# Second attention of a transformer block: where the softmax sums of each head are formed

## The chip, the cores and the metric

The kernel runs on one core of a Trainium2 chip. The metric is the device time of one execution in microseconds (us). The engines of the core work side by side, each through its own instructions in order, and wait for one another on semaphores: TensorE (PE in the profile, with its weight loads as PEld), VectorE (DVE), ScalarE (ACT), GpSimd (POOL) and SyncE (SP), which issues most of the transfers.

## The reference

`x` is 16 batches of 128 tokens of 128 numbers, with a context of 128 tokens of 96 numbers for each batch. Four stages follow one another, each on the layer norm of `x` (the last on `x` itself) and each added to `x`: an attention of 16 heads of 8, a mixture of 8 experts, a second attention of 16 heads of 64, and a mixture of 16 experts. The change is in the second attention:

```python
q_in = x @ Wq + _lora(x, q_down, q_up, q_alpha)
org_ctx = context[:, :end, :]            # 124 tokens
ipa_ctx = context[:, end:, :]            # 4 tokens
k_in = org_ctx @ Wk + _lora(org_ctx, k_down, k_up, k_alpha)
v_in = org_ctx @ Wv + _lora(org_ctx, v_down, v_up, v_alpha)
out = _attention(q_in, k_in, v_in)       # softmax over the 124 keys of each head
out_ipa = _attention(q_in, ipa_k, ipa_v) # softmax over the 4 keys of each head
out = out + IPA_SCALE * out_ipa
return out @ Wo + bo + _lora(out, o_down, o_up, o_alpha)
```

So for each batch, each of 128 queries has 16 rows of 124 powers, each divided by its own sum.

## The kernel before

The program is written engine by engine, with the order of each engine's instructions written out by hand. Every product is in fp32. The second attention runs in rounds, `round1(b)` for b from -1 to 16 (and from -4 on GpSimd, which has less to do in the early ones). A round does several batches at different stages at once: the scores and powers of batch b, the turning, the outputs and the projection of batch t = b - 1, the queries, keys and values of batch f = b + 1, and half of the first mixture's expert products of batch g = b + 4 in each of two places, while there is such a batch (up to b = 11). The rounds from 12 on carry pieces of the second mixture's routing instead: its hidden layer, its top 32 of 128 taken eight at a time (`eight`), and the gathering of rows by one-hot products (`tell`, `onehot`, `gather`, `gathered`).

The 16 heads of a batch are four groups n of CH = 4 heads. Scores of group n lie in PSUM bank n, 4 x 128 columns, of which 124 of each head are the original context and 4 the others. For each group:

- VectorE's `shifted(b, n)` (L755, L756, L758) takes the negated maximum of each head's 124 scores into `negmax1`, and shifts the 4 others into `ipa_s`.
- ScalarE's `powers(b, n)` (L1128) reads the bank and writes `p1`, one activation a head, since each head has its own shift as bias. The last of the four counts up `Z.exp`.
- VectorE's `summed(b, n)` waits for `Z.exp`, reduces the four heads' 496 powers to four sums (L772), waits for that, and takes their reciprocals (L774), which counts up `Z.rsum`.
- GpSimd's `norm(b, n)` (L496) waits for `Z.rsum` and multiplies the four heads' powers by them in place. In the next round TensorE's `turn` (L1491) transposes them, VectorE's `turned` (L766) copies them to `p1T`, and `outputs` (L1521) multiplies them with the values.

In VectorE's round `summed(b, 0)` stands after the second turned group, the other three stand together behind `weighted` (L728), and `ipa_norm` (L779, L781, L783) follows them. `powers` 0 and 1 of a round stand on ScalarE ahead of the copies of the queries (L1135, each after its group) and of `weighted` (L1090, four activations, half of a mixture product); `powers` 2 and 3 stand behind it, then the shifted ones' power (L1218), the outputs' copies (L1141), the keys' copy (L1235), the turned input (L1156) and the values' copies (L1146).

At the end of a round TensorE's projection (L1690) is taken by VectorE's residual (L304), and TensorE's first product of queries (L1500) in the next round, as bank 7 is used again, waits for that by `Z.x_new`. In the rounds b = -1, 3 and 7 (`head_of`) VectorE also does `head_weights` (L709 to L721) ahead of the residual: the choice of two experts for four batches. In the same rounds ScalarE's `head_turned` (L1077) stands behind `powers(b, 0)`, and TensorE's `head_logits` (L1428) waits for it. Rounds b = 2, 6, 10, 11 end with four normalizations in a row (L694, L619).

Of the kernel before, what the change touches and what calls it, by code (L numbers as in the profile page):

```python
# [8 lines left out]
ALU = mybir.AluOpType  # L9
ACT = mybir.ActivationFunctionType  # L10
X = mybir.AxisListType.X
# [9 lines left out]
ORG = S - IPA  # L21
# [6 lines left out]
CH = 4  # L28
# [4 lines left out]
def named(make, prefix, names):  # L33

    return type(prefix, (), {name: make(f"{prefix}_{name}") for name in names.split()})
# [16 lines left out]
def build_program(nc, T, out):  # L52

    with ExitStack() as ctx:
        def sb(name, shape, dt=F32):
            return ctx.enter_context(nc.sbuf_tensor(name, shape, dt))
# [13 lines left out]
        def blocks(b_, rows=128):  # L70
            return b_[0:rows, :].rearrange("p (g n) -> p g n", g=CH)
# [7 lines left out]
        stats = sb("stats", [128, B, 6])  # L79
# [4 lines left out]
        class Arena:  # L84
# [9 lines left out]
            def take(self, shape, dt=F32):  # L94
# [8 lines left out]
                if dt != F32:  # L103
# [71 lines left out]
        p1 = work.take([128, 2, CH, CH, S])  # L175
# [9 lines left out]
        negmax1 = sb("negmax1", [128, 2, H])  # L185
        sums1 = sb("sums1", [128, 2, H])
# [66 lines left out]

        W = named(sem, "w", "turned downT alpha ctx made taken added")
        Z = named(sem, "z", "xn xb tr xT q q_sb k0 k1 k0_sb k1_sb ki v v_sb vi0 vi1 score ipa_max maxed ipa_exp ipa_step ipa_p "
                            "exp sum rsum norm turned p_sb p_odd o o_sb proj x_new stats")

        R = named(sem, "r", "wide count tok picks xn tr xT hid th h logit max ex step topx top turned slot")
        G = named(sem, "g", "told oh got xg")
# [302 lines left out]
        def _(dve):  # L562
# [205 lines left out]
            def summed(b, n):  # L768

                dve.wait_ge(Z.exp, CH * b + n + 1)  # L770
                part = slice(CH * n, CH * n + CH)
                dve.tensor_reduce(sums1[:, b % 2, part], p1[:, b % 2, n, :, 0:ORG], X, ALU.add).then_inc(Z.sum, 1)  # L772
                dve.wait_ge(Z.sum, CH * b + n + 1)
                dve.reciprocal(rsum1[:, b % 2, part], sums1[:, b % 2, part]).then_inc(Z.rsum, 1)  # L774

            def ipa_norm(b):
# [83 lines left out]
            def round1(b):  # L860
# [13 lines left out]
                if there(b):  # L874
                    summed(b, 0)
# [36 lines left out]
                if there(b):  # L912
                    summed(b, 1)
                if b == 15:
                    onehot(3)
                if there(b):
                    summed(b, 2)
                    summed(b, 3)
                    ipa_norm(b)
# [114 lines left out]
        def _(act):  # L1034
# [89 lines left out]
            def powers(b, n):  # L1124

                act.wait_ge(Z.maxed, CH * b + n + 1)
                for c in range(CH):
                    ins = act.activation(p1[:, b % 2, n, c, 0:ORG], blocks(bank[n])[:, c, 0:ORG], ACT.Exp,  # L1128
                                         bias=negmax1[:, b % 2, CH * n + c:CH * n + c + 1])
                ins.then_inc(Z.exp, 1)  # L1130

            def queries(f, n):
# [48 lines left out]
            def round1(b):  # L1181
                f, t, g = b + 1, b - 1, b + 4
                if there(b):
                    powers(b, 0)
# [8 lines left out]
                if there(b):  # L1193
                    powers(b, 1)
# [8 lines left out]
                if there(b):  # L1203
                    powers(b, 2)
# [640 lines left out]
```

## Time and profile before

| | us |
|---|---|
| three runs | 531.68, 531.92, 533.07 |
| median | 531.92 |
| the profiled execution | 532.59 |
| its span in the trace | 530.90 |
| TensorE busy | 495.0 (93%) |
| VectorE busy | 397.5 (75%) |
| ScalarE busy | 272.2 (51%) |
| GpSimd busy | 235.7 (44%) |
| the second attention, rounds 0 to 15 | 141 to 402 on the span |

The profiled execution took 532.59 us; its trace spans 530.90 us of that, so 1.69 us lie around the span. Busy time is the sum of an engine's instructions where they do not overlap. Two instructions that follow one another on ScalarE or VectorE overlap a little, so the start of one to the start of the next (its pitch) is shorter than the duration. The granted clock of TensorE was full (1.00) in the whole second attention.

### The profile page before, as it was taken

Reading aid. Unit: us, or ns where it says so; the run is one execution under the profiler, and the core shown is the slowest. Engines: PE = TensorE matmul, PEld = TensorE weight load, DVE = VectorE, ACT = ScalarE, POOL = GpSimd, SP = SyncE. Lnnn points to the kernel's source line nnn. Section 1 sums busy time; section 2 is a strip of 40 time slices with the busy share of each in tenths; the row PEclk is TensorE's granted clock in tenths of the full one; section 3 lists DMA queues with packets and bytes.
Section 4 is the critical chain, followed back from the end, with each engine's and each line's share of the span. In section 5 each row is a group of like instructions: output and inputs, shape, how many; then the busy total and the mean of one; then the engine's idle time right before and its main releaser. Section 6 shows DMA issues by size and latency. Waiting matters only on the chain.

```text
span 530.9 us, 13371 instructions
## 1 busy us (share of the span) xinstructions
PE 495.0 (93%) x5113; PEld 380.4 (72%) x5113; DVE 397.5 (75%) x1064; ACT 272.2 (51%) x728; POOL 235.7 (44%) x331
## 2 busy tenths in 40 slices
PE   5799998889999998999989999999999999999996
PEld 4467665546567776777768777778857897789895
DVE  6788998556687789777897897777986678536553
ACT  3366564445475564657545665555663544514332
POOL 5844553025365525556255454633312890081440
PEclk9699999899999999999999999999999999999999
DMA  8900000000001101111000000021110400001001
GB/s 227 220 4 4 2 2 2 2 1 7 4 0 32 32 2 33 32 32 32 2 2 1 3 1 3 3 62 45 39 41 1 120 1 2 0 4 41 2 2 41
DMA packets 21871, 14.47 MB, mean 27 GB/s; under 512 B 5928, under 2 KB 21136, under 8 KB 21808
## 3 DMA queue, kind: packets, MB, share of 16 engines
q1 hardware_dynamic: 20704, 13.31, 9.1%
q8 instruction: 42, 0.69, 0.6%
q10 hardware_dynamic: 1104, 0.30, 0.3%
q14 instruction: 21, 0.17, 0.1%
HBM read 12.30 MB, written 1.05 MB: 25 GB/s over the span
## 4 chain that ended last, share of the span: by engine, by line
PE 73%; DVE 20%; issue 3%; ACT 2%; DMA 1%; POOL 0%; SPq 0%; DVEq 0%
PE bank L1758 9%; PE bank L1767 5%; PE bank L1352 5%; PE bank L1521 5%; PE bank L1433 4%; PE bank L1528 4%; PE bank L1508 4%; PE bank L1690 4%; PE bank L1480 4%; PE bank L1500 4%; PE bank L1491 3%; PE bank L1774 3%; PE bank L1337 3%; PE bank L1579 3%; DVE negmax L756 2%
## 5 line engine op out<-in xcount | busy, mean ns | idle before, releaser
L496 POOL TENSOR_TENSOR work<-work,rsum 128x496 f32<-128x496 f32 x64 | 64.2, 1015 | 131.6 <-DVE rsum L774 131.6
L1128 ACT ACTIVATE work<-bank,negmax 128x124 f32<-128x124 f32 x256 | 72.7, 378 | 77.6 <-DVE ipa_s L758 77.6
L531 POOL TENSOR_SCALAR work<-work,slot 128x128 f32<-128x128 f32 x64 | 49.8, 804 | 48.1 <-DVE slot L849 29.3
L1758 PE MATMUL bank<-work 128*128 128x256 f32 x224 | 53.4, 381 | 0.0
L993 DVE SCALAR_TENSOR_TENSOR work<-work,bank 128x256 f32<-128x256 f32 x64 | 26.9, 420 | 32.9 <-ACT work L1280 32.7
L479 POOL TENSOR_TENSOR work<-work 128x512 f32<-128x512 f32 (+2 forms) x48 | 40.3, 839 | 14.1 <-DVE work L728 11.6
L1280 ACT ACTIVATE work<-bank 128x256 f32<-128x256 f32 x64 | 24.6, 384 | 40.5 <-PE bank L1758 29.0
L1758 PEld LDWEIGHTS bank<-work 128*128 128x128 f32 x224 | 40.3, 190 | 4.7 <-DVE work L996 0.2
L430 POOL TENSOR_TENSOR rstd<-veps,minus_half 128x1 f32<-128x1 f32 (+3 forms) x28 | 21.1, 754 | 49.3 <-DVE veps L573 49.2
L756 DVE TENSOR_REDUCE negmax<-bank 128x4 f32<-128x496 f32 x64 | 42.3, 662 | 0.0
L627 DVE TENSOR_REDUCE negmax<-bank 128x8 bf16<-128x1024 f32 x32 | 39.1, 1221 | 4.3 <-PE bank L1322 3.6
L772 DVE TENSOR_REDUCE sums<-work 128x4 f32<-128x496 f32 x64 | 41.4, 647 | 0.5 <-ACT work L1128 0.5
L766 DVE COPY work<-bank 128x512 f32<-128x512 f32 x60 | 40.7, 678 | 0.8 <-PE bank L1491 0.8
L1500 PE MATMUL bank<-xT,work 128*128 128x128 f32 x256 | 34.6, 279 | 7.1 <-DVE x_all L304 4.1
L1480 PEld LDWEIGHTS bank<-work 64*128 64x128 f32 x512 | 31.1, 187 | 13.9 <-issue 8.9
L1491 PE MATMUL bank<-ident,work 128*128 128x128 f32 x256 | 40.1, 279 | 0.3 <-DVE work L783 0.3
L1069 ACT ACTIVATE work<-bank 128x1024 f32<-128x1024 f32 x32 | 31.0, 1022 | 13.8 <-PE bank L1337 13.8
L1480 PE MATMUL bank<-work 64*128 64x128 f32 x512 | 37.2, 285 | 1.0 <-issue 1.0
L1500 PEld LDWEIGHTS bank<-xT,work 128*128 128x128 f32 x256 | 31.1, 192 | 9.4 <-issue 4.7
L1521 PEld LDWEIGHTS bank<-work 128*64 128x64 f32 x512 | 27.4, 136 | 13.2 <-issue 10.4
L1690 PEld LDWEIGHTS bank<-work 128*128 128x128 f32 x256 | 31.0, 191 | 7.4 <-issue 5.1
L1521 PE MATMUL bank<-work 128*64 128x128 f32 x512 | 35.0, 279 | 0.6 <-DVE work L766 0.6
(197 smaller groups left out, 1086.3 us busy)
## 6 DMA issues: line engine op xcount, KB each, us to landing
work<-in_L_ffn_w_dram SPq DMA_DIRECT2D x42, 128.0 KB, 2.3
x_all<-in_x_dram SPq DMA_DIRECT2D x4, 256.0 KB, 5.5
out_dram<-x_all SPq DMA_DIRECT2D x4, 256.0 KB, 2.5
ctx_all<-in_ctx_dram SPq DMA_DIRECT2D x4, 192.0 KB, 5.7
ctx_all<-in_L_ffn_w_dram SPq DMA_DIRECT2D x6, 128.0 KB, 2.2
work<-in_L_xattn_Wq_dram SPq DMA_DIRECT2D x1, 512.0 KB, 6.4
work<-in_L_xattn_Wo_dram SPq DMA_DIRECT2D x1, 512.0 KB, 8.5
work<-in_L_ffn_We_dram SPq DMA_DIRECT2D x1, 512.0 KB, 6.0
```

The lines of the kernel that those rows point to most:

```text
L496: pool.tensor_tensor(part, part, rsum1[:, b % 2, CH * n:CH * n + CH].unsqueeze(2).broadcast_to((128, CH, ORG)), ALU.mult).then_inc(Z.norm, 1)
L531: ins = pool.tensor_scalar(ohw_of(e)[:, k, :], count[:, :], slot[:, h, 0, k, e % E1:e % E1 + 1], slot[:, h, 1, k, e % E1:e % E1 + 1], ALU. ...
L756: dve.tensor_reduce(negmax1[:, b % 2, part], got_s[:, :, 0:ORG], X, ALU.max, negate=True)
L766: dve.tensor_copy(p1T[:, CH * n:CH * n + CH, :], blocks(bank[(4, 6, 5, 4)[n]])).then_inc(Z.p_sb, 1)
L772: dve.tensor_reduce(sums1[:, b % 2, part], p1[:, b % 2, n, :, 0:ORG], X, ALU.add).then_inc(Z.sum, 1)
L1128: ins = act.activation(p1[:, b % 2, n, c, 0:ORG], blocks(bank[n])[:, c, 0:ORG], ACT.Exp, bias=negmax1[:, b % 2, CH * n + c:CH * n + c + 1])
L1480: mm = pe.matmul(blocks(bank[2 * half + odd])[:, c, :], q1T[rows, b % 2, CH * half + c, :], k1T[rows, b % 2, CH * half + c, :], start=True ...
L1491: mm = pe.transpose(blocks(bank[(4, 6, 5, 4)[n]])[:, c, :], p1[:, t % 2, n, c, :], ident[:, :])
L1500: mm = pe.matmul(blocks(bank[5 - n])[:, c, :], wq1[:, part], xT[:, f % 2, :], start=True, stop=True)
L1521: mm = pe.matmul(blocks(bank[5 - n])[D1 * odd:D1 * odd + D1, c, :], v1[:, t % 2, D1 * h:D1 * h + D1], p1T[:, CH * (2 * n + odd) + c, :], s ...
L1690: mm = pe.matmul(bank[7][:, 0:D], o1T[:, c, :], wo1[:, c, :], start=(c == 0), stop=(c == 7))
L1758: mm = pe.matmul(halves(bank[4 + c])[:, n, :], up_weights(e, n, c), xgT[e // E1][:, :, e % E1, :], start=True, stop=True)
```

## The change

Each power's activation gets a second output: `accum_out`, the sum of what it writes along the row, which goes to its head's place in `sums1`. VectorE's reduction of the four heads' powers goes, with the wait for it; the reciprocal of the four sums stays, behind the same wait for `Z.exp`. The semaphore `Z.sum` is dropped. Lines above the edit keep their numbers; L774 becomes L772, and L1128 becomes L1127.

```diff
@@ -769,8 +769,6 @@
                 dve.wait_ge(Z.exp, CH * b + n + 1)
                 part = slice(CH * n, CH * n + CH)
-                dve.tensor_reduce(sums1[:, b % 2, part], p1[:, b % 2, n, :, 0:ORG], X, ALU.add).then_inc(Z.sum, 1)
-                dve.wait_ge(Z.sum, CH * b + n + 1)
                 dve.reciprocal(rsum1[:, b % 2, part], sums1[:, b % 2, part]).then_inc(Z.rsum, 1)
@@ -1125,8 +1123,9 @@
                 act.wait_ge(Z.maxed, CH * b + n + 1)
                 for c in range(CH):
+                    h = CH * n + c
                     ins = act.activation(p1[:, b % 2, n, c, 0:ORG], blocks(bank[n])[:, c, 0:ORG], ACT.Exp,
-                                         bias=negmax1[:, b % 2, CH * n + c:CH * n + c + 1])
+                                         bias=negmax1[:, b % 2, h:h + 1], accum_out=sums1[:, b % 2, h:h + 1])
                 ins.then_inc(Z.exp, 1)
```

VectorE before, from the half mixture product of round 3 to the first step of `head_weights`:

```order
L728 TENSOR_TENSOR work<-bank,work 128x512 [waits f_x_new,f_yb]
L772 TENSOR_REDUCE sums<-work 128x4 [waits z_exp]
L774 RECIPROCAL rsum<-sums 128x4 [waits z_sum]
...
L779 TENSOR_REDUCE ipa_sum<-ipa_s 128x16 [waits z_ipa_exp]
L781 RECIPROCAL ipa_sum<-ipa_sum 128x16 [waits z_ipa_step]
L783 TENSOR_TENSOR work<-ipa_s,ipa_sum 128x16x4 [waits z_ipa_step]
L709 TENSOR_TENSOR work<-work 128x256
```

VectorE in the changed kernel, the same place:

```order
L728 TENSOR_TENSOR work<-bank,work 128x512 [waits f_x_new,f_yb]
L772 RECIPROCAL rsum<-sums 128x4 [waits z_exp] x3
L777 TENSOR_REDUCE ipa_sum<-ipa_s 128x16 [waits z_ipa_exp]
L779 RECIPROCAL ipa_sum<-ipa_sum 128x16 [waits z_ipa_step]
L781 TENSOR_TENSOR work<-ipa_s,ipa_sum 128x16x4 [waits z_ipa_step]
L709 TENSOR_TENSOR work<-work 128x256
```

The three pairs of reduction and reciprocal (two of them behind the dots) have become three reciprocals in a row; nothing else changed places.

ScalarE before, from the first powers of round 1 to the shifted ones' power:

```order
L1128 ACTIVATE work<-bank,negmax 128x124 x4
L1135 ACTIVATE work<-bank 128x512
...
L1090 ACTIVATE work<-bank,work 128x128 x4
L1128 ACTIVATE work<-bank,negmax 128x124 x8
L1218 ACTIVATE ipa_s<-ipa_s 128x64
```

ScalarE in the changed kernel, the same place:

```order
L1127 ACTIVATE work,sums<-bank,negmax 128x124 x4
L1134 ACTIVATE work<-bank 128x512
...
L1088 ACTIVATE work<-bank,work 128x128 x4
L1127 ACTIVATE work,sums<-bank,negmax 128x124 x8
L1217 ACTIVATE ipa_s<-ipa_s 128x64
```

The order and the number of the rows on ScalarE are those of before; the powers have a second output, `sums`.

## Rows read from the trace of the kernel before

**Rows 1.** The page: busy time, share of the span and instructions of each engine.

```profile
PE 495.0 (93%) x5113; PEld 380.4 (72%) x5113; DVE 397.5 (75%) x1064; ACT 272.2 (51%) x728; POOL 235.7 (44%) x331
```

**Rows 2.** Waits of TensorE, 141 to 402 us: total us, times, longest.

```profile
PE bank L1500 <- DVE x_all L304: 4.1, 2, 2.0
PE bank L1500 <- DVE work L766: 3.0, 6, 1.0
PE bank L1428 <- ACT work L1077: 1.5, 2, 0.7
PE bank L1579 <- DVE work L857: 1.3, 2, 0.9
...
PE bank L1491 <- DVE work L783: 0.3, 1, 0.3
```

**Rows 3.** The page's costliest groups: busy us, mean ns of one, idle before.

```profile
L1128 ACT ACTIVATE work<-bank,negmax 128x124 f32<-128x124 f32 x256 | 72.7, 378 | 77.6 <-DVE ipa_s L758 77.6
L772 DVE TENSOR_REDUCE sums<-work 128x4 f32<-128x496 f32 x64 | 41.4, 647 | 0.5 <-ACT work L1128 0.5
```

**Rows 4.** Timeline, VectorE and TensorE, end of round 3: start us, us, instruction.

```profile
196.83 0.66 DVE L772 TENSOR_REDUCE sums<-work 128x4 f32<-128x496 f32 x1
197.52 0.18 DVE L774 RECIPROCAL rsum<-sums 128x4 f32<-128x4 f32 x1
197.61 0.64 DVE L772 TENSOR_REDUCE sums<-work 128x4 f32<-128x496 f32 x1
...
199.15 0.19 DVE L779 TENSOR_REDUCE ipa_sum<-ipa_s 128x16 f32<-128x64 f32 x1
...
206.37 1.16 PE L1500 MATMUL bank<-xT,work 128*128 128x128 f32 x8 [2.05 <-DVE x_all L304]
```

**Rows 5.** Timeline, ScalarE, last powers of round 3; then groups by shape.

```profile
195.16 1.13 ACT L1128 ACTIVATE work<-bank,negmax 128x124 f32<-128x124 f32 x4 [0.21 <-DVE ipa_s L758]
196.17 0.27 ACT L1218 ACTIVATE ipa_s<-ipa_s 128x64 f32<-128x64 f32 x1
196.31 0.24 ACT L1082 ACTIVATE work<-work 128x32 f32<-128x32 f32 x1
...
L1096 ACT ACTIVATE alpha<-alpha 128x4 f32<-128x4 f32 x1 | 0.2, 207 | 0.0
```

**Rows 6.** Timeline, TensorE and ScalarE, round 9, which stands for nine plain ones.

```profile
291.51 1.13 ACT L1128 ACTIVATE work<-bank,negmax 128x124 f32<-128x124 f32 x4 [3.15 <-DVE ipa_s L758]
...
294.45 1.22 ACT L1090 ACTIVATE work<-bank,work 128x128 f32<-128x128 f32 x4
...
297.12 1.02 PE L1433 MATMUL bank<-work 128*128 128x512 f32 x2
...
299.21 0.60 ACT L1141 ACTIVATE work<-bank 128x512 f32<-128x512 f32 x1 [0.33 <-PE bank L1521]
...
301.21 1.12 PE L1528 MATMUL bank<-work,cT_all 96*124 96x512 f32 x2
```

**Rows 7.** Timeline, TensorE, ScalarE, VectorE, round 0.

```profile
146.57 1.21 ACT L1090 ACTIVATE work<-bank,work 128x128 f32<-128x128 f32 x4
...
147.84 1.12 PE L1433 MATMUL bank<-work 128*128 128x512 f32 x2
...
155.61 1.13 PE L1500 MATMUL bank<-xT,work 128*128 128x128 f32 x8 [0.36 <-DVE work L766]
```

**Rows 8.** Timeline, rounds 12, 14 and 15.

```profile
342.24 0.61 ACT L1162 ACTIVATE work<-bank 128x512 f32<-128x512 f32 x1
342.91 1.12 PE L1546 MATMUL bank<-work 128*128 128x512 f32 x2
...
378.50 1.09 PE L1521 MATMUL bank<-work 128*64 128x128 f32 x16 [0.35 <-DVE work L766]
...
395.03 0.62 ACT L1178 ACTIVATE work<-bank 128x512 f32<-128x512 f32 x1
...
396.08 0.38 PE L1571 MATMUL bank<-work,b_pick 128*128 128x512 bf16 x1
```

More of the change, by code:

```diff
@@ L255, in build_program @@
         Z = named(sem, "z", "xn xb tr xT q q_sb k0 k1 k0_sb k1_sb ki v v_sb vi0 vi1 score ipa_max maxed ipa_exp ipa_step ipa_p "
-                            "exp sum rsum norm turned p_sb p_odd o o_sb proj x_new stats")
+                            "exp rsum norm turned p_sb p_odd o o_sb proj x_new stats")
         R = named(sem, "r", "wide count tok picks xn tr xT hid th h logit max ex step topx top turned slot")
```

## The prediction

> **What bounds the kernel now.** The busy shares come first: TensorE is busy 93% of the span, VectorE 75%, ScalarE 51% [rows 1]. A change that moves work from VectorE to ScalarE can thus gain at most TensorE's waits for VectorE, and loses where ScalarE becomes the one waited for. The waits of TensorE in the second attention [rows 2] show what there is. The two largest, 2.05 us each, are L1500 behind VectorE's residual, in the rounds that follow 3 and 7, where VectorE comes late out of its long end of round [rows 4]. Six of 3.0 us in all are for the turned powers' copy L766. These follow the chain projection, residual, norm, maxima, copy, which starts with TensorE's own projection, so an earlier VectorE does not help them, except where VectorE was late for the residual. Two of 0.74 us are L1428 behind ScalarE's L1077, which stands right behind a group of powers: they can only grow. Two of 1.3 us together, in round 15, are gathers behind one-hot rows of VectorE, with sums among its work.
>
> **What goes.** 64 reductions of 647 ns, 41.4 us of VectorE [rows 3]. Most of it lies beside a busy TensorE: in a plain round VectorE waits for the projection at the round's end anyway. It is on the path where VectorE is late:
> - Rounds 3 and 7. From the first of the three late reductions at 196.83 to L779 at 199.15 are 2.32 us [rows 4]. Three reciprocals stay. The row after one starts 0.09 us behind it, and its whole duration is 0.18; I take 3 x 0.18 = 0.54, as each waits on a semaphore. So 1.78 us go, less than the 2.05 that TensorE waits. Behind the residual the L766 wait stays.
> - Round 14: L1521's wait of 0.35 us [rows 8] goes, since the reduction ahead of it in VectorE's queue takes more.
> - Round 15: of the gathers' 1.3 us [rows 2], one reduction, 1.78 / 3 = 0.59 us.
> - Round 0: its waits, 0.28 for L783 [rows 2] and 0.36 for L766 [rows 7], go, 0.64 us.
>
> Sum: 2 x 1.78 + 0.35 + 0.59 + 0.64 = 5.1 us, if the sums cost ScalarE nothing.
>
> **What is added: e, the price of one sum.** No row of before shows an accumulator output. The changed order has the same number of ScalarE's rows, each power with a second output, which would allow e = 0; that the engine needs a step of its own to write 128 single numbers out is as possible. The nearest rows are ScalarE's smallest activations [rows 5]. L1218 (64 elements) starts at 196.17, the next at 196.31: a pitch of 0.14 us, of which the elements are 0.04 to 0.07, as one of 64 takes 0.27 and one of 32 takes 0.24. So about **0.09 us** is what a step with hardly any elements adds in a queue, and that I take. The upper bound: it takes all of L1096's 207 ns and overlaps with nothing, which also loses the 0.12 us by which a power's 378 ns exceeds its pitch of 0.25 (four take 1.01 us from 195.16 to 196.17): e = 0.33. A gain below nothing is excluded, since the powers' own work stays. Per group of four, d = 4e: forecast 0.36, ends 0 and 1.3 us.
>
> The Trainium skill, in "VectorE: DVE Perf Modes", section "Two Vector instructions with no wait between them", says that a VectorE instruction which also writes out its accumulator is two instructions, the second a read of the accumulator. If ScalarE does so as well, e = 0 falls away, and the change puts 256 instructions on ScalarE for 64 taken from VectorE. No row of before shows this.
>
> **Where ScalarE's added time is hidden and where not.** ScalarE's total grows by 256 x 0.09 = 23 us, on 272 of 531 [rows 1], so its sum is no bound; order is. In the plain round 9 [rows 6], with TensorE's times fixed:
> - L1090 ends at 295.67 and lies behind two groups; the product L1433 that reuses its bank starts at 297.12. Slack 1.45 against 2d: no wait up to d = 0.72.
> - Groups 2 and 3 follow it (1.02 us each by pitch), then L1218. L1141 could be done at 298.37 + 4d. The values' product L1528 needs its bank at 301.21: no wait up to d = 0.71. Beyond it the round loses 4d - 2.84.
>
> At 0.36 nine plain rounds lose nothing. What has no such cover:
> - Rounds 3 and 7: L1077 comes d later, and TensorE and VectorE with it. The gain of 1.78 becomes 1.78 - 0.36 = 1.42. From d = 0.47 on VectorE's third late reciprocal also waits for the powers themselves.
> - Round 0: L1090 ends at 147.78, its product starts at 147.84 [rows 7]: 2d = 0.72 late, against the 0.64 above. Net cost 0.08.
> - Round 12: L1162 ends at 342.85, its product starts at 342.91 [rows 8]: d less 0.06, 0.3 us.
> - Round 15: L1178 ends at 395.65, behind four groups; L1571 starts at 396.08 [rows 8]. 4d - 0.43 = 1.0, of which ScalarE's idle gaps between the groups take most; I take 0.3 (an estimate).
>
> **The sum.** 2 x 1.42 + 0.35 + 0.59 = 3.8 gained; 0.08 + 0.3 + 0.3 = 0.7 lost; **3.1 us net**. GpSimd gets its sums' reciprocals earlier and loses nothing; the first mixture and the routing after 402 us do not change. The profiled execution of 532.59 us would become 529.5; the median of 531.92 lies 0.67 below it and becomes **528.8**.
>
> **Rivals.**
> 1. *ScalarE becomes the bound of each round* (slower). The mechanism is 4d - 2.84 in nine plain rounds, with the product L1528 waiting for L1141 in place of nothing. It decides from d = 0.71, e = 0.18. At e = 0.20, d = 0.8: nine times 0.36 is 3.2; rounds 0, 12 and 15 cost 1.0 + 0.7 + 1.8; rounds 12 to 14 some 0.5; the gains shrink to 1.3 in rounds 3 and 7 and 0.9 elsewhere. Net +5.0: 536.9. At e = 0.25 it is about +15 (547), at the upper bound about +33 (565). For it: a sum must be complete before it is written, so it may well wait for the power's end. Against it: small activations follow at 0.14 us.
> 2. *The sum is free* (d = 0): -5.1 us, 526.8. For it speaks the unchanged count of rows.
> 3. *No change worth measuring*: e between 0.14 and 0.18, where gains of about 2.5 meet losses of 1.5 to 3, or VectorE is no earlier in rounds 3 and 7, since its steps there share GpSimd's time (L783 took 0.70 us beside it). 531.5.
>
> **How the numbers follow.** The forecast (e from 0.04 to 0.14) has 0.50, the free sum 0.10, no change 0.16, ScalarE as bound 0.24. Faster or slower by over 0.3%, 1.6 us, is what a measurement of this kernel can tell from no change. Faster is 0.50 + 0.10 = 0.60, same 0.16, slower 0.24. The range runs from the free sum, 526.0 with 0.8 for the estimates in it, to rival 1 at e = 0.20, 537.0; above that I leave some 0.15.
>
> **What would show it.** In the profile after: rows of L1127 as groups of about 1.5 us for four, against 1.13; VectorE's busy time near 356 us; L1500 waiting for the residual near 0.6 us instead of 2.05; L1428 waiting for L1077 near 1.1 instead of 0.74; no wait of L1433 for L1090 nor of L1528 for L1141 in plain rounds. If these two appear, d is above 0.7 and rival 1 holds. If L1500 still waits 2 us, the step on the late VectorE is wrong.

## The result

The changed kernel takes a median of 528.06 us (526.16 to 528.28, four runs) against 531.9 us (531.68 to 533.07), a ratio of 0.9908 with a 95% interval of 0.9883 to 0.9932. A second series, six runs beside others of the kernel before, gave 527.51 us and 0.989 (0.9865 to 0.9914). It is faster by 4 to 6 us, where 3.1 were forecast; the median lies 0.7 us from the forecast time and inside the range.

The page after: span, busy time and the costliest groups of ScalarE's powers (busy us, mean ns of one, idle before), to be laid beside [rows 1, 3].

```profile
span 524.4 us, 13559 instructions
...
PE 493.0 (94%) x5109; PEld 380.0 (72%) x5113; DVE 353.4 (67%) x1000; ACT 290.8 (55%) x984; POOL 235.6 (45%) x331
```

```profile
L1127 ACT ACTIVATE work<-bank,negmax 128x124 f32<-128x124 f32 x256 | 90.2, 390 | 58.7 <-DVE ipa_s L758 58.6
L1127 ACT ACTIVATION_READ_ACCUMULATOR work<-bank,negmax 128x1 f32 x256 | 59.7, 233 | 0.0
```

VectorE lost 64 instructions and 44 us, ScalarE gained 256 instructions and only 18.6 us. The 59.7 us of the second row are no such cost: each of these rows overlaps with the power ahead of it and the one behind it. The stretch of TensorE's waits shows what it was worth. After, 141 to 402 us (total us, times, longest), beside [rows 2]:

```profile
PE bank L1427 <- ACT work L1075: 1.9, 2, 1.0
PE bank L1499 <- DVE work L766: 1.4, 4, 0.7
PE bank L1479 <- issue: 1.0, 1, 1.0
PE bank L1420 <- DVE work L694: 0.9, 2, 0.5
PE bank L1432 <- ACT work L1088: 0.8, 1, 0.8
PE bank L1578 <- DVE work L855: 0.6, 2, 0.4
PE bank L1527 <- ACT work L1234: 0.4, 1, 0.4
PE bank L1570 <- ACT work L1150: 0.4, 1, 0.4
PE bank L1520 <- DVE work L766: 0.3, 1, 0.3
...
PE bank L1545 <- ACT work L1161: 0.2, 1, 0.2
```

The residual's two waits of 2.05 us are gone altogether. With them went 1.6 of 3.0 us of waits for the copy L766 and 0.7 of 1.3 us of the gathers' waits in round 15. New are five small waits for ScalarE, 2.2 us together: 0.4 more for L1075, those of L1432 and L1527 in round 0, of L1545 in round 12 and of L1570 in round 15.

**A measure finer than the time.** All the code up to round 0 is the same in every kernel here, but for one small memset in the kernel without sums, and yet the first power of round 0 starts anywhere between 141.7 and 145.8 us in the profiled executions. That scatter is as large as the effect. So below I also give the stretch from the first power to the end of the span: 387.27 us before, 381.55 after (and 381.67 in the second series). By it the change gains 5.7 and 5.6 us. Each stretch is that of one profiled execution; the two of the changed kernel differ by 0.12 us. "Gain" without more means this stretch against that of before.

### The profile page after: what moved, and what is told of

Same layout as the page of the kernel before. It is cut to its first block, busy times and chain, and to the rows that moved or that the text cites. A ratio compares the mean times of both kernels' runs of the same rounds, so it can differ in the third digit from the quotient of the medians.

```text
span 524.4 us, 13559 instructions
## 1 busy us (share of the span) xinstructions
PE 493.0 (94%) x5109; PEld 380.0 (72%) x5113; DVE 353.4 (67%) x1000; ACT 290.8 (55%) x984; POOL 235.6 (45%) x331
## 4 chain that ended last, share of the span: by engine, by line
PE 77%; DVE 13%; ACT 4%; issue 3%; DMA 1%; ACTq 1%; POOL 1%; DVEq 0%; POOLq 0%
PE bank L1757 9%; PE bank L1520 5%; PE bank L1766 5%; PE bank L1351 5%; PE bank L1527 5%; PE bank L1689 5%; PE bank L1507 5%; PE bank L1479 5%; PE bank L1432 4%; PE bank L1499 4%; PE bank L1490 4%; PE bank L1773 3%; PE bank L1578 3%; PE bank L1336 2%; ACT work L1127 2%
## 5 line engine op out<-in xcount | busy, mean ns | idle before, releaser
L1127 ACT ACTIVATE work<-bank,negmax 128x124 f32<-128x124 f32 x256 | 90.2, 390 | 58.7 <-DVE ipa_s L758 58.6
L496 POOL TENSOR_TENSOR work<-work,rsum 128x496 f32<-128x496 f32 x64 | 65.0, 1026 | 123.9 <-DVE rsum L772 123.9
L1127 ACT ACTIVATION_READ_ACCUMULATOR work<-bank,negmax 128x1 f32 x256 | 59.7, 233 | 0.0
L479 POOL TENSOR_TENSOR work<-work 128x512 f32<-128x512 f32 (+2 forms) x48 | 39.6, 824 | 14.1 <-DVE work L728 11.6
L766 DVE COPY work<-bank 128x512 f32<-128x512 f32 x60 | 40.7, 678 | 0.8 <-PE bank L1490 0.8
L304 DVE TENSOR_TENSOR x_all<-bank,x_all 128x128 f32<-128x128 f32 x16 | 4.7, 291 | 51.5 <-PE bank L1689 49.0
L1499 PE MATMUL bank<-xT,work 128*128 128x128 f32 x256 | 34.4, 278 | 1.5 <-DVE work L766 1.4
```

The source lines that it names most:

```text
L479: pool.tensor_tensor(y[:, 0:half, :], y[:, 0:half, :], y[:, half:2 * half, :], ALU.add).then_inc(F.sum, 1)
L496: pool.tensor_tensor(part, part, rsum1[:, b % 2, CH * n:CH * n + CH].unsqueeze(2).broadcast_to((128, CH, ORG)), ALU.mult).then_inc(Z.norm, 1)
L766: dve.tensor_copy(p1T[:, CH * n:CH * n + CH, :], blocks(bank[(4, 6, 5, 4)[n]])).then_inc(Z.p_sb, 1)
L1499: mm = pe.matmul(blocks(bank[5 - n])[:, c, :], wq1[:, part], xT[:, f % 2, :], start=True, stop=True)
```

## The experiments

Most kernels differ from one of the two by two predicates, of the round b and the group of heads n. They decide who makes the sums of a group:

```
 act.activation(..., bias=negmax1[...],
+    **({'accum_out': sums1[:, b % 2, h:h + 1]} if by_act(b, n) else {}))
 # VectorE, in the loop of groups, ahead of the reciprocal
+if by_dve(b, n):
+    dve.tensor_reduce(sums1[:, b % 2, part], p1[:, b % 2, n, :, 0:ORG], X, ALU.add).then_inc(Z.sum, 1)
+    dve_sums.append(0)
+    dve.wait_ge(Z.sum, len(dve_sums))
```

### Both the old sums and the new: what ScalarE's part costs alone

```
+by_act = True; by_dve = True   # VectorE's sums go to an array nobody reads
```

> ScalarE gives the sums, and VectorE makes its reductions too, into a place that nobody reads. Theory A (the gain is VectorE's time, ScalarE's 0.34 us pitch per power and sum is nearly hidden): only the costs stay, some 0.7 us in round 0, 0.3 in each of rounds 3 and 7, 0.2 to 0.4 in each of rounds 10 to 12, up to 1 in round 15, so 533 to 535. Theory B (the gain is from something else that comes with the new output, such as shifted starts on GpSimd): faster than before, 528 to 531.

Measured: 536.44 us (534.89 to 537.28), ratio 1.0075 (1.0046 to 1.0105). The stretch loses 3.5 us, but some 1.6 of these stem from round 3, where TensorE's granted clock averaged 0.91 and 0.81, so that for part of these 12 us it was 1.2 GHz and not 2.4. The same products run in round 7 of this execution at a full clock (1.00 from 254 to 266 us); why it fell in round 3 is not shown. The windows (length, busy us and count of TensorE, its loads, VectorE, ScalarE and GpSimd, then the granted clock):

```profile
186.00:192.00 6.00, 4.67 (x33) 4.25 (x34) 5.17 (x18) 4.17 (x19) 1.40 (x2) 0.91 0.02 3
192.00:198.00 6.00, 6.00 (x44) 3.83 (x44) 3.06 (x9) 3.62 (x18) 0.00 (x0) 0.81 0.00 0
```

Without that piece the loss is near 2 us. The time is above the expected 533 to 535, 4.1 us over the kernel before in its series; one trace cannot say whether the other executions held such a piece too. Theory B is out. So by the trace the powers' second output costs about 2 us where nothing is taken away from VectorE, and none of it falls into the plain rounds: the residuals of the rounds behind 3 and behind 7 lie as far apart as before.

### No sums at all: the other half alone

```
+by_act = False; by_dve = False   # sums1 is set to 1.0 once, before round 0
```

This kernel leaves the sums of the second attention's powers out.

> Leaves the sums out altogether: neither ScalarE nor VectorE forms them, the reciprocals are of ones, so the powers are not divided. Theory A: this is the change with its price on ScalarE at zero; rounds 3 and 7 give 2.4 us each (all that TensorE waited there), round 14 0.85, round 0 0.6, round 15 0.5: 525 to 526, some 1.5 us under the change. Theory C (ScalarE's sums cost nothing even where nothing covers them): the time of the change, 527 to 528.

Measured: 524.16 us (521.92 to 526.57), ratio 0.9842 (0.9806 to 0.9878); the stretch gains 8.0 us. The time is 0.8 us below the expected range, as the price on ScalarE had been put at 1.5. Against the changed kernel's 5.7 the stretch puts ScalarE's whole cost at **2.3 us**, which agrees with the 2.2 us of new waits above. The ceiling of what freeing VectorE can bring is 8 us, where the forecast's terms came to 5.1.

### Only where VectorE is late, and everywhere but there

```
+by_act = b in (3, 7, 14) and n >= 1;         by_dve = not by_act   # first kernel
+by_act = not (b in (3, 7) and n >= 1);       by_dve = not by_act   # second kernel
```

> The change for groups 1 to 3 of rounds 3, 7 and 14 alone, 9 of 64 reductions. Theory A: nearly the whole gain, 2 x 2.4 + 0.85 = 5.6 us, and none of the costs in rounds 0, 3, 7 (group 0), 12 and 15: 526 to 527. Theory D (the gain is spread over all rounds): 9/64 of it, 531.

> The change everywhere but in groups 1 to 3 of rounds 3 and 7, 58 of 64 reductions gone. Theory A: 2 x 2.4 us of the gain go and what is left is round 14 against the costs: 531 to 532. Theory D: 58/64 of the gain, 528.4.

Measured: 528.47 us (524.45 to 528.77), ratio 0.9901 (0.9864 to 0.9939), a gain of 5.4 us in the stretch; and 533.1 us (530.45 to 535.18), ratio 1.0019 (0.9996 to 1.0042), a gain of 0.4. Both times lie 1 to 1.5 us above what was expected, the gain of the first in the stretch 0.2 below it. Nine of the 64 reductions carry nearly all of the changed kernel's net gain. With six of them put back, the residual's wait is back, here at the head of TensorE's waits (141 to 402 us) and in the timeline of round 4 of the second kernel:

```profile
PE bank L1512 <- DVE x_all L304: 4.3, 2, 2.3
```

```profile
205.04 1.16 PE L1512 MATMUL bank<-xT,work 128*128 128x128 f32 x8 [2.26 <-DVE x_all L304]
```

In round 4 it is 2.26 us, 0.2 more than the 2.05 of [rows 4]: in that one round VectorE stops for 0.25 us in the choice of experts ahead of the residual. In round 8 it is 2.04, as before. This settles where the net gain sits.

### The price of a sum doubled and trebled

The changed kernel with one, then with two activations of a single column behind each power. They read the array of maxima, and nobody reads what they write.

```
 act.activation(..., accum_out=sums1[:, b % 2, h:h + 1])
+for k in range(1):     # first kernel;  range(2) in the second
+    ins = act.activation(extra[:, k, ...], negmax1[:, b % 2, h:h + 1], ACT.Copy)
```

> The changed kernel with one more small activation (128x1, to a place that nobody reads) behind each power, which doubles what ScalarE is given: about 0.09 to 0.1 us each, d = 0.72 to 0.8 per group against 0.36. Theory A (4d - 2.84 per plain round from d = 0.71): 0 to 0.4 us in each of nine plain rounds, 0.5 to 1 us more in rounds 0, 3, 7, 12 and 15 each: 530 to 535. Theory G (ScalarE has room for a second one, as it is busy 55%): 528 to 529.

> The changed kernel with two more small activations (128x1, to a place that nobody reads) behind each power: the step behind a power costs 0.09 to 0.1 three times, d = 1.1 per group. Theory A (4d - 2.84 per plain round): 1.6 us in each of nine plain rounds, where one extra activation cost 0.16, so 14 us there, and 4 to 7 more in the other rounds: 546 to 552. Theory G (the cost grows in proportion to ScalarE's added work, from 3 us at one extra): 540 to 542.

Measured: 534.75 us (532.82 to 537.61), ratio 1.0028 (1.0001 to 1.0056); and 556.71 us (554.97 to 559.18), ratio 1.0458 (1.0388 to 1.0527). Timeline of ScalarE in the first kernel, start and duration in us:

```profile
143.73 0.36 ACT L1128 ACTIVATE work<-bank,negmax 128x124 f32<-128x124 f32 x1 [5.29 <-DVE ipa_s L759]
143.99 0.19 ACT L1128 ACTIVATION_READ_ACCUMULATOR work<-bank,negmax 128x1 f32 x1
144.08 0.19 ACT L1131 ACTIVATE extra<-negmax 128x1 f32<-128x1 f32 x1
144.17 0.35 ACT L1128 ACTIVATE work<-bank,negmax 128x124 f32<-128x124 f32 x1
```

The accumulator's read and the added activation each take 0.09 us of the queue, so the pitch of a power, the start of one to the start of the next, goes from 0.34 to 0.44 us, and to 0.53 in the second kernel. Four powers take 1.74 and 2.12 us against the 1.01 of [rows 5], so d is 0.73 and 1.11 us. The prediction's condition for a plain round, no loss up to d = 0.71 and 4d - 2.84 behind it, gives 0.08 and 1.60. A plain round of the first kernel lasts 15.73 us against 15.57, a loss of 0.16; one of the second lasts 17.11, a loss of 1.54. Both executions also have two pieces at a lower clock, in rounds 0 and 7 (0.69 to 0.74 in the first kernel, 0.77 to 0.94 in the second); the plain rounds compared here lie outside them. The first time is inside its range. The second is 4.7 us above its own, though the plain rounds lost what was expected: the first two rounds alone lost 4.7 us, and in round 7 the lower clock cost 1.6. In the second kernel the waits named for the plain round have come:

```profile
PE bank L1530 <- ACT work L1143: 6.3, 10, 1.0
PE bank L1435 <- ACT work L1089: 5.0, 10, 2.2
```

So rival 1 was a real mechanism with its threshold in the right place to within a tenth of a microsecond a round; the changed kernel, at d = 0.36, stays at half of it.

### GpSimd moved instead of the sums

The gain at rounds 3 and 7 came out larger than the sums taken away there. Those rounds also hold the choice of experts on VectorE, nine small operations behind `ipa_norm`, which run beside GpSimd's scaling of the powers (L496) and its weighted sums of the experts (L479). This kernel is the one before, no sum moved; GpSimd starts two of its sums of experts only when VectorE has finished that choice.

```
 def experts_sum(g):
+    if g in (7, 11):
+        pool.wait_ge(F.step, HEAD_STEPS * ((g + 1) // 4 + 1))
```

> The kernel before, but GpSimd starts the additions for batches 7 and 11 only when VectorE has finished its choice of experts in rounds 3 and 7; no sum moves. Theory E (part of VectorE's late end of round is GpSimd's work on the same SBUF port): L709 and L710 take 0.4 us each instead of 1.25 and 1.38, the choice of experts 4.0 instead of 5.7, and rounds 3 and 7 gain about 1.5 us each: stretch 384.2, about 529. Theory F (VectorE's steps are long for another reason): they keep their times, and the time stays at 532.

Measured: 529.67 us (528.29 to 532.95), ratio 0.9935 (0.9912 to 0.9958), a gain of 2.4 us in the stretch, out of one wait that is met twice. The choice of experts at the end of round 3, VectorE and GpSimd, in this kernel:

```profile
199.56 1.25 DVE L711 TENSOR_TENSOR work<-work 128x256 f32<-128x256 f32 x1
200.84 0.43 DVE L712 TENSOR_TENSOR work<-work,lower 128x256 f32<-128x256 f32 x1
201.31 0.42 DVE L714 TENSOR_TENSOR work<-work 128x256 f32<-128x256 f32 x1
201.76 0.42 DVE L715 TENSOR_TENSOR work<-work 128x256 f32<-128x256 f32 x1
...
203.56 0.29 DVE L304 TENSOR_TENSOR x_all<-bank,x_all 128x128 f32<-128x128 f32 x1
203.60 2.61 POOL L481 TENSOR_TENSOR work<-work 128x512 f32<-128x512 f32 x3 [3.08 <-DVE work L723]
```

The kernel before, same stretch:

```profile
200.28 1.25 DVE L709 TENSOR_TENSOR work<-work 128x256 f32<-128x256 f32 x1
201.21 2.92 POOL L479 TENSOR_TENSOR work<-work 128x512 f32<-128x512 f32 x3
201.56 1.38 DVE L710 TENSOR_TENSOR work<-work,lower 128x256 f32<-128x256 f32 x1
202.98 0.83 DVE L712 TENSOR_TENSOR work<-work 128x256 f32<-128x256 f32 x1
203.84 0.56 DVE L713 TENSOR_TENSOR work<-work 128x256 f32<-128x256 f32 x1
...
206.02 0.29 DVE L304 TENSOR_TENSOR x_all<-bank,x_all 128x128 f32<-128x128 f32 x1
```

The same operation on the same shape takes 0.42 us with GpSimd standing still and 0.56 to 1.38 beside it, and the piece from the first of these rows to the residual shrinks from 5.74 to 4.00 us. The first of the four is still slow in this kernel, since it stands beside GpSimd's scaling of the powers, which was not moved; the expectation had missed that. The moved sums cost something too: they now stand beside the normalization behind the residual (L299 takes 0.86 us instead of 0.33). The residual comes 1.75 us earlier, and 0.5 of that is lost at the next one, which leaves 1.2 a round where 1.5 were expected.

### The moved wait on top of the change

> The changed kernel again, beside the others of this set. Every theory: 526 to 528.5; from the first power to the end of the trace 381.5 us, 5.7 less than before, of which rounds 3 and 7 hold 2.6 each.

> The changed kernel, and GpSimd starts the additions for batches 7 and 11 only when VectorE has finished its choice of experts in rounds 3 and 7. Theory A with E (both edits shorten the same late stretch of VectorE, and TensorE waited only 2.46 us there): VectorE's choice of experts shrinks from 5.2 to about 4 us, but rounds 3 and 7 gain at most the 0.2 us that TensorE still waits, so 526 to 528, the stretch from the first power to the end 381.2 to 382. If the gains add up: another 2.4 us, stretch 379.2.

Measured: 527.51 us as told under the result, and with GpSimd's wait added 527.32 us (525.72 to 528.68), ratio 0.9881 (0.9817 to 0.9945); the stretch gains 6.1 us against 5.7. The wait that gave 2.4 us alone gives 0.4 here. Both edits make VectorE earlier at the same two residuals. After the change TensorE no longer waits there; what was left to gain was the 0.2 us that it still waited for L766 in each of rounds 4 and 8, and that is gone in this kernel.

### Only the groups that pay, and the best version

The choice reads off the experiments: ScalarE makes the sums where VectorE was late or its sum stood ahead of something waited for, and in no group of rounds 0, 12 and 15, where ScalarE has no slack.

```
+by_act = (b in (3, 7, 9, 10, 11) and n >= 1) or b == 14;  by_dve = not by_act
```

The second kernel of this pair is the same with GpSimd's wait.

> ScalarE gives the sums where it paid: groups 1 to 3 of rounds 3, 7, 9, 10 and 11 and all of round 14; VectorE reduces elsewhere. Theory A: the gains of rounds 3 and 7 (5.1 in all), 10 and 11 (0.4) and 14 (0.85) without the costs of rounds 0, 12 and 15: from the first power to the end 380.9 us, 6.3 less than before; 525.5 to 528. Theory D (gain in proportion to the reductions removed): 19 of 64, 530.5.

> Both edits that paid: ScalarE gives the sums in groups 1 to 3 of rounds 3, 7, 9, 10 and 11 and in all of round 14, and GpSimd starts the additions for batches 7 and 11 behind VectorE's choice of experts. Theory A with E: what the chosen sums gained without the clock dip in their trace (6.6 us from the first power to the end) and 0.3 in each of rounds 3 and 7: 379.5 to 380.5 against 387.3 before, 525 to 528. If the second edit takes back what the first gave: 381.5 or more.

Measured: 527.63 us (525.78 to 529.45), ratio 0.9887 (0.9859 to 0.9914); and **524.74 us** (522.8 to 526.47), ratio 0.9835 (0.9802 to 0.9869), the fastest kernel here that computes everything. The first one's stretch gains only 4.7 us, because in round 0, where its code is that of before, the granted clock averaged 0.72, so that it was partly at 1.2 GHz and else at 2.4:

```profile
143.00:150.00 7.00, 7.00 (x43) 5.71 (x43) 3.94 (x15) 4.90 (x16) 1.01 (x1) 0.72 0.02 4
```

It cost 1.8 us at the first residual; without them the gain is 6.6 us, 0.9 more than the change's. By time alone this kernel can't be told from the changed one. The second gains 7.1 us in a stretch at the full clock, 1.0 more than the changed kernel with the same wait; its time is 0.3 us below the expected range.

## Why the prediction was right, and where its sizes were off

**The bound and the side: right.** TensorE sets the time, VectorE's sums were on the path at the ends of rounds 3 and 7, and the other 55 sums gave little more than they cost. The kernel that moves nine of them shows it (5.4 of 5.7 us), and the one that moves all but six of them loses it. That the median came within 0.7 us of the forecast is in part luck: by the stretch the gain is 5.7 us where 3.1 were forecast, and the medians of the two series differ by 3.8 and 6.1.

**The price of a sum: right to 0.01 us, and not for free.** ScalarE, start of round 3 after:

```profile
186.47 0.36 ACT L1127 ACTIVATE work<-bank,negmax 128x124 f32<-128x124 f32 x1 [4.18 <-DVE ipa_s L758]
186.73 0.19 ACT L1127 ACTIVATION_READ_ACCUMULATOR work<-bank,negmax 128x1 f32 x1
186.82 0.35 ACT L1127 ACTIVATE work<-bank,negmax 128x124 f32<-128x124 f32 x1
...
187.84 0.61 ACT L1075 ACTIVATE work<-bank 128x512 f32<-128x512 f32 x1
...
188.50 1.06 PE L1427 MATMUL bank<-work 128*128 128x8 f32 x8 [0.96 <-ACT work L1075]
```

Four powers take 1.37 us from 186.47 to 187.84 against 1.01 in [rows 5]: d = 0.36, as forecast (the "about 1.5 us" for four was the same number with the last row's tail in it). The read is a row of its own, which the order of instructions ahead of the run does not list; rival 2, the free sum, falls with it. By the rule of the Trainium skill, "VectorE: DVE Perf Modes", section "Two Vector instructions with no wait between them", an accumulator output makes two instructions of one on VectorE, the second a read. The page speaks of VectorE alone; this trace shows the same on ScalarE, with 256 added rows of 0.23 us in the mean. ScalarE's 2.3 us of cost, split by the residuals of this kernel against those of the one without sums: about 1.1 in round 0 (charged at 0.72), 0.35 in each of rounds 3 and 7 (0.36), and 0.6 in rounds 12 to 15 (0.6), of which 0.1 is back by the end of the span. Round 0 cost more than was charged because TensorE waits there not only for L1088 (0.79) but also for the keys' copy L1234 (0.39), which the forecast did not have.

**Plain rounds: right.** L1088 and L1140, once L1090 and L1141, make TensorE wait in none of them. Round 9 after is as long as before.

**Rounds 3 and 7, the term that was mis-sized.** Forecast 1.42 us each; the residual comes 2.61 and 2.60 us earlier, of which 0.2 is given back at the next one, since TensorE then sets the pace: 2.4 each. VectorE after, end of round 3 (the reciprocals' line is still L772):

```profile
195.81 0.68 DVE L728 TENSOR_TENSOR work<-bank,work 128x512 f32<-128x512 f32 x1
196.40 0.29 DVE L772 RECIPROCAL rsum<-sums 128x4 f32<-128x4 f32 x3
196.62 0.18 DVE L777 TENSOR_REDUCE ipa_sum<-ipa_s 128x16 f32<-128x64 f32 x1
...
197.66 0.42 DVE L709 TENSOR_TENSOR work<-work 128x256 f32<-128x256 f32 x1
198.11 0.42 DVE L710 TENSOR_TENSOR work<-work,lower 128x256 f32<-128x256 f32 x1
198.57 1.12 DVE L712 TENSOR_TENSOR work<-work 128x256 f32<-128x256 f32 x1
199.73 1.12 DVE L713 TENSOR_TENSOR work<-work 128x256 f32<-128x256 f32 x1
...
202.86 0.29 DVE L304 TENSOR_TENSOR x_all<-bank,x_all 128x128 f32<-128x128 f32 x1
...
205.42 1.13 PE L1499 MATMUL bank<-xT,work 128*128 128x128 f32 x8 [0.20 <-DVE work L766]
```

Three things lie between 1.42 and the 2.6 at the residual, and a fourth belongs to them:
- *The reciprocals.* Three start at 196.40 and the next row at 196.62, so they take 0.22 us and not the 0.54 charged: +0.32. [Rows 4] had shown the pitch of 0.09 us behind one, and I took the duration instead.
- *GpSimd's contention.* The choice of experts, L709 to the residual, takes 5.20 us against 5.74: +0.54. It starts earlier and so meets GpSimd's work elsewhere: L709 and L710 take 0.42 us where they took 1.25 and 1.38, but L712 and L713 take 1.12 each where they took 0.83 and 0.56. This came by timing alone, so it is luck, and the kernel that only moves GpSimd shows that such an overlap is worth microseconds. Rival 3 had named the overlap, as something that takes gain away; it added. L781 gives another 0.08.
- *The delay by ScalarE.* Charged at d = 0.36, it was 0.13 at VectorE's late steps: TensorE does wait 0.96 us for L1075 instead of 0.74, but not all of that reaches VectorE. +0.23.
- *The wait behind the residual.* I wrote that the wait for L766 stays. In round 4 it was 0.41 us before (row below) and is 0.20 now. That is inside the 2.4, not added to it; it shows that the cap of 2.05 us on each gain was too low.

Together the first three give 1.42 + 0.32 + 0.62 + 0.23 = 2.59, the 2.6 measured at the residual, and less 0.2 the 2.4 kept.

**The small terms.** Round 14 was forecast at 0.35 and gave 0.85. The wait forecast, L1521's, lies behind group 0's sum, and without it TensorE's work of the round comes 0.6 us earlier. The last three groups' sums give the other 0.26, as they do in the kernel that moves only them: in the kernel before they made VectorE late for the residual, straight behind L836, and after it waits for TensorE. That second part was not in the forecast. Before, then after:

```profile
375.05 0.65 DVE L772 TENSOR_REDUCE sums<-work 128x4 f32<-128x496 f32 x1
...
385.30 0.69 DVE L836 TENSOR_TENSOR work<-top_at_f,e_mask 128x512 bf16<-128x512 f32 x1
385.91 0.28 DVE L304 TENSOR_TENSOR x_all<-bank,x_all 128x128 f32<-128x128 f32 x1
```

```profile
379.44 0.29 DVE L304 TENSOR_TENSOR x_all<-bank,x_all 128x128 f32<-128x128 f32 x1 [0.59 <-PE bank L1689]
```

Round 15 was forecast at 0.59 - 0.3 and gave nothing: the gathers' 0.7 us of [rows 2] did go, and ScalarE took as much. Round 0 cost 0.23 against 0.08 (0.9 gained, 1.1 lost). Round 12 cost 0.11 net against 0.3: ScalarE took 0.35, and 0.24 were gained that the forecast did not have, as the chosen groups' kernel shows, where round 12 has no sum on ScalarE. Rounds 10 and 11 gained 0.15 and 0.24, where none was forecast; a wait of 0.28 us for L766 in round 10 of the kernel before is absent after. The two waits of before, round 4 and round 10:

```profile
208.37 1.13 PE L1500 MATMUL bank<-xT,work 128*128 128x128 f32 x8 [0.41 <-DVE work L766]
...
308.38 1.13 PE L1500 MATMUL bank<-xT,work 128*128 128x128 f32 x8 [0.28 <-DVE work L766]
```

In sum, rounds 3 and 7 brought 2.0 us more than forecast, and the rest some 0.6 more.

**What the signs told.** Of those named, VectorE's busy time (353.4 against 356), the absence of the two waits of a plain round, and L1427's longest wait of 0.96 (1.1) came. L1499's wait for the residual was to be 0.6 and is none, for the reasons above.

## What to carry over

Count an accumulator output as an instruction of its own with its pitch in the queue, and give it only to the groups where the other engine is late and this one has slack: 9 of 64 sums brought nearly all of this gain, and leaving out the groups that did not pay for themselves gave 0.9 us more. When an engine is late at one place, look first at what stretches its operations there. Here one wait on a third engine gave 2.4 us without moving a sum, though two edits that relieve the same late step hardly add up.

## What the runs showed of the hardware

- ScalarE's accumulator read is a row of 0.19 to 0.35 us, 0.23 in the mean, which overlaps with its neighbours: the queue grows by 0.09 us, as it does for an activation of a single column. The read's row starts 0.10 us ahead of the end of its power's (186.73 against 186.83), so the step that the prediction feared, a wait for the full end, is not there.
- VectorE's 128x256 operation with two operands takes 0.42 us with GpSimd standing still and up to 1.38 us beside it, some three times as long. Where a gain is timed to tenths of a microsecond, this counts beside the removed work: 0.54 us against 2.10 at the end of round 3.
- TensorE's granted clock fell at places that differ between executions (means of 0.91 and 0.81 in round 3 of one kernel, 0.72 in round 0 of another), at 1.6 to 1.8 us each. With the start's scatter of 4 us they are why the stretch behind a common first instruction tells more than the time. They do not explain the start's scatter by themselves: the earliest start, 141.7 us, has a piece at 0.50 ahead of it (18 to 24 us). How much of the spread of 2 to 7 us between runs of one kernel is the clock's, no run here settles.
